# Closing a row block of a graph layer: a 32x32 turn-back on VectorE with statistics added over quadrants, in place of TensorE transposes

## The reference, cut to what matters

```python
# x: 8192 x 256, adj: 8192 x 8192, w: 256 x 256, all float32
xw  = max(sign(x), 0) @ sign(w).T
out = relu(adj @ xw)
y   = x + out
result = (y - mean(y)) / sqrt(var(y) + 1e-5)     # along the 256 columns of each row
```

## Time and profile before

| | us |
|---|---|
| three runs: median | 991.02 |
| three runs: lowest, highest | 989.96, 991.04 |
| the profiled execution | 990.72 |
| span of its instructions | 988.9 |
| TensorE busy in it | 972.6 (98%) |
| VectorE busy | 846.8 (86%) |
| GpSimd busy | 841.8 (85%) |
| ScalarE busy | 614.2 (62%) |

### The profile page before, as it was taken

The page is one execution under the profiler, slowest core; times in us unless marked ns, Lnnn a source line. Parts: engine busy times, 40 slices in busy tenths (PEclk is TensorE's granted clock), DMA queues, the critical chain, the costliest instruction groups (busy, mean ns, idle before and its releaser), DMA issues.

```text
span 988.9 us, 12529 instructions
## 1 busy us (share of the span) xinstructions
PE 972.6 (98%) x4612; PEld 810.2 (82%) x4612; DVE 846.8 (86%) x879; ACT 614.2 (62%) x657; POOL 841.8 (85%) x362
## 2 busy tenths in 40 slices
PE   5999999999999999999999999999999999999997
PEld 5978888888888888888888888888888888888886
DVE  5777988989888898988989898898988989898894
ACT  3777675665656566565665656566565656656563
POOL 3567998988889899888998889899888998889893
PEclk9999999999999999999999999999999999999999
DMA  9999999999999999999999999999999999999971
GB/s 300 348 349 326 318 314 283 323 324 285 326 287 309 283 321 312 287 316 308 287 302 298 330 287 301 310 294 317 293 316 277 310 285 322 326 287 308 320 185 43
DMA packets 296701, 294.70 MB, mean 298 GB/s; under 512 B 9664, under 2 KB 296640, under 8 KB 296640
## 3 DMA queue, kind: packets, MB, share of 16 engines
q1 hardware_dynamic: 156640, 155.21, 57.0%
q10 hardware_dynamic: 140000, 138.69, 49.8%
HBM read 285.47 MB, written 8.39 MB: 297 GB/s over the span
## 4 chain that ended last, share of the span: by engine, by line
PE 96%; DMA 1%; DVE 1%; ACT 1%; ACTq 1%; issue 0%; POOL 0%; DVEq 0%
PE ps L617 91%; PE ps L691 1%; PE ps L611 1%; DMA raw<-in_adj_dram 1%; PE ps L593 1%; PE ps L655 1%; ACTq L194 1%; ACT hi L324 0%; PE ps L583 0%; DVE turned L444 0%; POOL lo L304 0%; ACT xw L317 0%; ACTq L187 0%; PE ps L679 0%; DVE ps L444 0%
## 5 line engine op out<-in xcount | busy, mean ns | idle before, releaser
L304 POOL TENSOR_TENSOR lo<-turned,hi 128x1024 fp32r<-128x1024 f32 x351 | 838.6, 2411 | 118.3 <-ACT hi L324 114.4
L617 PE MATMUL ps<-hi,xw 128*128 128x512 f32 x1984 | 774.4, 390 | 0.5 <-ACT xw L317 0.5
L617 PE MATMUL ps<-lo,xw 128*128 128x512 f32 x1984 | 772.2, 389 | 0.0
L324 ACT ACTIVATE hi<-turned 128x1024 fp32r<-128x1024 f32 x351 | 372.6, 1062 | 254.8 <-PE ps L617 173.4
L617 PEld LDWEIGHTS ps<-hi,xw 128*128 128x128 f32 x1984 | 372.5, 188 | 77.8 <-ACT xw L317 1.1
L617 PEld LDWEIGHTS ps<-lo,xw 128*128 128x128 f32 x1984 | 372.5, 188 | 76.7
L444 DVE STREAM_TRANSPOSE turned<-raw 128x1024 f32<-128x1024 f32 x351 | 425.1, 1218 | 1.2 <-DMA raw<-in_adj_dram 1.2
L448 DVE TENSOR_TENSOR lo<-ps,hi 128x1024 fp32r<-128x1024 f32 x161 | 196.6, 1221 | 111.0 <-ACT hi L324 111.0
L324 ACT ACTIVATE hi<-ps 128x1024 fp32r<-128x1024 f32 x161 | 165.1, 1026 | 89.5 <-PE ps L617 77.2
L444 DVE STREAM_TRANSPOSE ps<-raw 128x1024 f32<-128x1024 f32 x161 | 196.4, 1220 | 3.0 <-DMA raw<-in_adj_dram 2.9
L341 ACT ACTIVATE rows<-rows,shift,rstd 128x256 f32<-128x256 f32 x62 | 36.2, 586 | 1.6 <-DVE shift L467 1.6
(11 more groups left out here) (39 smaller groups left out, 131.9 us busy)
## 6 DMA issues: line engine op xcount, KB each, us to landing
raw<-in_adj_dram SPq DMA_DIRECT2D x250, 512.0 KB, 11.0
raw<-in_adj_dram ACTq DMA_DIRECT2D x250, 512.0 KB, 12.0
rows<-in_x_dram SPq DMA_DIRECT2D x16, 512.0 KB, 10.8
out_dram<-rows SPq DMA_DIRECT2D x15, 512.0 KB, 15.9
raw<-in_adj_dram SPq DMA_DIRECT2D x12, 256.0 KB, 8.7
raw<-in_adj_dram ACTq DMA_DIRECT2D x12, 256.0 KB, 9.4
x_sb<-in_x_dram SPq DMA_DIRECT2D x10, 256.0 KB, 10.6
x_sb<-in_x_dram ACTq DMA_DIRECT2D x10, 256.0 KB, 11.1
```

Of the source, the lines that this page charges most:

```text
L304: pool.tensor_tensor(lo[:, n % RING], turned[:, ordinal(n) % TP], hi[:, n % RING].bitcast(f32), ALU.subtract).then_inc(p_los_made, 1)
L324: act.activation(hi[:, n % RING], src, ACT.Copy).then_inc(his_made, 1)
L617: return pe.matmul(acc[b % 2][a], xw[:, step, a * P:(a + 1) * P], part[:, n % RING, k * MB:(k + 1) * MB], start=(step == 0 and part is hi) ...
```

## The change

The ending of the blocks 0 to 14 is made anew; block 15 keeps its own, with its columns in another order.

- The columns of `sign_wT` are put in another order, so that half `a` of the features holds, for each quadrant q of the partitions, the columns 64q + 32a to 64q + 32a + 31. VectorE turns the sums back in 32x32 squares, in one instruction from PSUM to SBUF (u = 7). Partition (q, r) then holds a quarter (64 columns) of the rows 32t + r, for t = 0 to 15.
- At u = 8 relu and the sum with x are one instruction (128x1024, both inputs in SBUF). x is loaded by quadrants: four DMAs of 128 KB per block, two from SyncE and two from ScalarE, in runs of 256 bytes; the result is stored likewise. There are two buffers in turns: the old `rows` and a new `rows_e`.
- Statistics are first taken of 64 columns each (16 small instructions at u = 9 to 12), and then TensorE adds over the quadrants with a 128x128 matrix `quads`: means behind unit 8, variances behind unit 16, two float32 matmuls of 16 columns each. Between them VectorE has four small instructions, at u = 16, 17 and 18.
- ScalarE loses its two relus; the standard deviations come at u = 23, and 16 normalising operations of 64 columns at u = 27 to 30.
- TensorE loses the 8 transposes of each ending, and the last unit of a block runs its products in the order of the others.

The core of the diff (the tail's waits, the semaphores and the allocation of buffers are left out):

```diff
+    C4 = D // G
+    MEANS_AT, VARS_AT = 8, 16
...
+    x_quads = x.rearrange("(b t r) (q c) -> b q r t c", t=NT, r=Q, q=G)
+    out_quads = out.rearrange("(b t r) (q c) -> b q r t c", t=NT, r=Q, q=G)
...
+        def load_quads(eng, b, side):
+            if b >= 2:
+                eng.wait_ge(quads_stored[b % 2], b // 2 * G * 16)
+            elif b == 0:
+                eng.wait_ge(signs_turned, 1)
+            else:
+                eng.wait_ge(xw_made, GROUPS)
+            for q in side:
+                eng.dma_start(rows_q[b % 2][q * Q:(q + 1) * Q], x_quads[b, q]).then_inc(quads_loaded[b % 2], 16)
+
+        def store_quads(eng, b, side):
+            eng.wait_ge(blocks_done, b + 1)
+            for q in side:
+                eng.dma_start(out_quads[b, q], rows_q[b % 2][q * Q:(q + 1) * Q]).then_inc(quads_stored[b % 2], 16)
...
SyncE, for b in 1..15, for c in 0..7, behind load_chunk:
-                    if c == 2 and b >= 2:
-                        store_rows(b - 2)
-                    if c == 3:
-                        load_rows(b - 1)
+                    if c == 0:
+                        load_quads(sp, b - 1, LOWER)
+                    if c == 3 and b >= 2:
+                        store_quads(sp, b - 2, LOWER)
...
ScalarE:
             def ending(b, u):
-                if u == RING - 1:
-                    make_relu(b)
-                if u == 18:
-                    make_std(b, slice(0, MT))
-                if 22 <= u < 22 + MT:
-                    normalise(b, u - 22, u - 22 == MT - 1)
+                if u == 23:
+                    act.wait_ge(vars_summed, b + 1)
+                    act.activation(std_q[:], sum_vars, ACT.Sqrt, bias=eps[:], scale=1.0 / Q).then_inc(stds_made, 1)
+                if 27 <= u < 31:
+                    act.wait_ge(shifts_made, b + 1)
+                    for t in range((u - 27) * G, (u - 26) * G):
+                        row = rows_q[b % 2][:, t]
+                        done = act.activation(row, row, ACT.Identity, bias=shift_q[:, t:t + 1], scale=rstd_q[:, t:t + 1])
+                    if u == 30:
+                        done.then_inc(blocks_done, 1)
+                if u == 31:
+                    store_quads(act, b, UPPER)
...
+                if n % UB == 20 and n // UB < NBLK - 1:
+                    load_quads(act, n // UB, UPPER)
...
VectorE:
             def ending(b, u):
...
+                if u == 7:
+                    dve.wait_ge(units_used, (b + 1) * UB)
+                    dve.wait_ge(sums_made, b)
+                    dve.transpose(flat[0].rearrange("p (t a j) -> p a t j", t=NT, a=DH), pair[b % 2]).then_inc(sums_turned, 1)
+                if u == 8:
+                    dve.wait_ge(sums_turned, b + 1)
+                    dve.wait_ge(quads_loaded[b % 2], (b // 2 + 1) * G * 16)
+                    dve.scalar_tensor_tensor(out=rows_q[b % 2], in0=back_q, scalar=0.0, in1=rows_q[b % 2],
+                                             op0=ALU.max, op1=ALU.add).then_inc(sums_made, 1)
+                if 9 <= u < 13:
+                    dve.wait_ge(sums_made, b + 1)
+                    for t in range((u - 9) * G, (u - 8) * G):
+                        dve.bn_stats(stats_q[:, t], rows_q[b % 2][:, t]).then_inc(stats_made, 1)
+                if u == 16:
+                    dve.wait_ge(means_summed, b + 1)
+                    for e in range(2):
+                        last = dve.tensor_tensor(dev_q[:, :, e], stats_q[:, :, 1 + 3 * e], sum_means, ALU.subtract)
+                    last.then_inc(devs_made, 1)
+                if u == 17:
+                    dve.wait_ge(devs_made, b + 1)
+                    dve.tensor_tensor(sq_q[:], dev_q[:], dev_q[:], ALU.mult).then_inc(squares_made, 1)
+                if u == 18:
+                    dve.wait_ge(squares_made, b + 1)
+                    dve.scalar_tensor_tensor(out=dev_q[:], in0=sq_q[:], scalar=float(Q), in1=parts,
+                                             op0=ALU.mult, op1=ALU.add).then_inc(parts_made, 1)
...
(u == 25: reciprocal of std_q; u == 26: shift_q from sum_means and rstd_q)
...
+            def make_quads():
+                dve.wait_ge(idents_made, 2)
+                dve.tensor_reduce(quad[:], ident[:].rearrange("p (q r) -> p r q", q=G), mybir.AxisListType.X,
+                                  ALU.add).then_inc(quad_made, 1)
+                dve.wait_ge(quad_made, 1)
+                for q in range(G):
+                    last = dve.tensor_scalar(quads[:, q * Q:(q + 1) * Q], quad[:], 1.0 / (G * 2), None, ALU.mult)
+                last.then_inc(quads_made, 1)
...
+                if n == UB - 2:
+                    make_quads()
...
TensorE:
-            def turn_back(b):
...
+            def add_means(b):
+                if b == 0:
+                    pe.wait_ge(quads_made, 1)
+                pe.wait_ge(stats_made, (b + 1) * NT)
+                if b:
+                    pe.wait_ge(shifts_made, b)
+                for e in range(2):
+                    last = pe.matmul(sum_means, quads[:], stats_q[:, :, 1 + 3 * e], start=(e == 0), stop=(e == 1))
+                last.then_inc(means_summed, 1)
+
+            def add_vars(b):
+                pe.wait_ge(parts_made, b + 1)
+                if b:
+                    pe.wait_ge(stds_made, b)
+                for e in range(2):
+                    last = pe.matmul(sum_vars, quads[:], dev_q[:, :, e], start=(e == 0), stop=(e == 1))
+                last.then_inc(vars_summed, 1)
...
-                if n >= UB and n % UB == BACK_AT:
-                    turn_back(n // UB - 1)
+                if n >= UB and n % UB == MEANS_AT:
+                    add_means(n // UB - 1)
+                if n >= UB and n % UB == VARS_AT:
+                    add_vars(n // UB - 1)
```

More of the change, by code:

```diff
@@ L105, in build @@
         shift = sb("shift", [P, MT], f32)
+        quad = sb("quad", [P, Q], f32)
+        quads = sb("quads", [P, P], f32)
+        stats_q = sb("stats_q", [P, NT, 6], f32)
+        dev_q = sb("dev_q", [P, NT, 2], f32)
+        sq_q = sb("sq_q", [P, NT, 2], f32)
+        std_q = sb("std_q", [P, NT], f32)
+        rstd_q = sb("rstd_q", [P, NT], f32)
+        shift_q = sb("shift_q", [P, NT], f32)
         eps = sb("eps", [P, 1], f32)
         warm = sb("warm", [P, 1], f32)
+        rows_q = [rows_e[:], rows[:].rearrange("p m d -> p (m d)").rearrange("p (t c) -> p t c", t=NT)]
         flat = [t.rearrange("p a b -> p (a b)") for t in (relu[:], rows[:])]
@@ L117, in build @@
         acc = [[ps[:, (2 * h + a) * BANK:(2 * h + a + 1) * BANK] for a in range(DH)] for h in range(2)]
+        pair = [ps[:, 2 * h * BANK:(2 * h + 2) * BANK].rearrange("p (a t r) -> p a t r", a=DH, t=NT) for h in range(2)]
+        sum_means, sum_vars = (ps[:, b * BANK:b * BANK + NT] for b in (6, 7))
         back = ps[:, 6 * BANK:8 * BANK].rearrange("p (m d) -> p m d", m=MT)
@@ L131, in build @@
         adj_loaded = [sem(f"adj_loaded{s}") for s in range(SLOTS)]
+        quads_loaded = [sem(f"quads_loaded{i}") for i in range(2)]
+        quads_stored = [sem(f"quads_stored{i}") for i in range(2)]
         rows_loaded = sem("rows_loaded")
@@ L281, in _ @@
                              rows[:, ms[0]:ms[-1] + 1]).then_inc(rows_stored, 16)
-            sp.wait_ge(rows_stored, (NBLK + 1) * 16)
+            sp.wait_ge(rows_stored, 2 * 16)
+            for i in range(2):
+                sp.wait_ge(quads_stored[i], (NBLK - i) // 2 * G * 16)
             sp.wait_ge(tile_stored, 16)
@@ L324, in make_hi @@
                 act.activation(hi[:, n % RING], src, ACT.Copy).then_inc(his_made, 1)
[L326 to L333, removed]
             def make_std(n, ms):
-                act.wait_ge(mvs_made, n + 1)
+                act.wait_ge(mvs_made, n - NBLK + 2)
                 act.activation(std[:, ms], mv[:, ms, 1], ACT.Sqrt, bias=eps[:]).then_inc(stds_made, 1)
@@ L409, in _ @@
             dve.wait_ge(w_negs, 1)
[L410 removed]
+            dve.scalar_tensor_tensor(out=sign_w, in0=w_sb, scalar=0.0, in1=w_neg,
                                      op0=ALU.is_gt, op1=ALU.subtract).then_inc(signs_made, 1)
@@ L470, in ending @@
             def ending(b, u):
-                whole = slice(0, MT)
-                if u == 13:
-                    dve.wait_ge(relus_turned, (b + 1) * MT)
-                    dve.wait_ge(rows_loaded, (b + 1) * 16)
-                    add_rows(whole)
-                if u == 14:
-                    for m in range(MT):
-                        make_stats(b, m)
-                if u == 15:
-                    dve.wait_ge(stats_made, (b + 1) * MT)
-                if u == 16:
-                    for m in range(MT):
-                        last = make_mv(m)
-                    last.then_inc(mvs_made, 1)
@@ L485, in ending @@
-                if u == 20:
-                    make_rstd(b, whole)
-                if u == 21:
-                    make_shift(b, whole)
+                means, parts = stats_q[:, :, 1::3], stats_q[:, :, 2::3]
```

(17 more changed lines are left out.)

61 lines of the change are left out of this document (29 added, 32 removed).

## The result

| us | before | changed |
|---|---|---|
| median of the runs | 990.94 | 1042.32 |
| lowest, highest | 989.96, 991.04 | 1029.74, 1054.38 |
| profiled execution | 990.72 | 1054.38 |
| span | 988.9 | 1052.6 |
| TensorE busy | 972.6 (98%) | 998.0 (95%) |

The changed kernel is slower: ratio 1.040, 95% interval [1.0379, 1.042], some 40 us. The forecast was 988.4 (982 to 1001).

The account below looks back on a forecast made before the run. TensorE, 98% busy and 96% of the chain, was taken as the bound: 990.72 - 4.7 (transposes out, small matmuls in) + 2.1 (block 1's wait) = 988.1, plus 0.30 to the median, forecast 988.4 us, range 982 to 1001.

Parts of the forecast that it names:

- four DMA issues, behind running activations: nothing: On ScalarE: the four DMA issues it gets per block stand behind running activations and cost no time.
- DMA: On the DMA queues: 256-byte runs take 3.5 us more per block, hidden by 8.6 us that are free.
- the 9 us more of the prediction: On the DMA engines: if a 256-byte run costs 47 ns like a whole one, 12.0 us per block instead of 3.0.
- the rival built on it: DMA becomes the bound: 9 us more against about 8 free, 1 to 1.6 per block, 1003 to 1010 us; chance 0.05.
- A pair of small matmuls: On TensorE: two float32 matmuls of 16 columns cost 0.28 us with the return, two pairs 0.56 per block.
- float32 in several passes: Rival on TensorE: four passes make a pair 0.87 us, total 1006; two passes 0.95 per block, 994; chance 0.17.
- the 4.7 us to be gained: On TensorE: transposes of 0.875 us per block replaced by matmuls of 0.56, saving 4.7 us over 15 blocks.
- Block 1: VectorE comes out of block 0 late, so TensorE waits behind unit 8: 2.1 us lost, once.
- VectorE's burst: From the turn of unit 7 to the last statistic VectorE issues 13.4 us of work; no wait in steady blocks.
- 0.6 for GpSimd: In steady blocks, VectorE's relu-and-sum waits 0.6 us for a GpSimd instruction to end, leaving a margin of 0.6.
- T0: The moment at which TensorE starts a block's unit 0, from which the prediction counts a block's times.
- The sum's upper bound: Upper of the forecast sum's own bounds, 983 and 994 us, for the whole kernel.

Follow-up runs that it names:

- f3: Changed kernel with the same eight DMAs per block in runs of 4 KB instead of 256 bytes: 995.7 us, ratio 1.0043 to the kernel before.
- f2: Changed kernel with the means asked for behind unit 10 instead of 8: 1029.4 us, ratio 1.0403 to the kernel before.
- g3: Changed kernel with all loads of x in runs of 4 KB, all stores still at 256 bytes: 1009.5 us, ratio 1.0192 to the kernel before.
- f1: Changed kernel with all eight small DMAs per block issued by SyncE, none by ScalarE: 1114.5 us, from 1087 to 1134.
- h2: Changed kernel with all eight DMAs per block in runs of 512 bytes: 996.4 us, ratio 1.006 to the kernel before.
- k1: Kernel before, plus eight added DMAs of 128 KB per block in runs of 256 bytes at the change's places: 1111.4 us, from 1085 to 1123.
- j3: Changed kernel with all small DMAs on SyncE and 20 of a block's 32 adj loads on ScalarE: 1204 us, from 1152 to 1224.
- g2: Changed kernel with SyncE's small DMAs in runs of 4 KB, ScalarE's still at 256 bytes: 1096.7 us, ratio 1.1077 to the kernel before.
- h3: Changed kernel with ScalarE's four small DMAs put at units apart: 1016 us, from 1007 to 1026, ratio 1.0175 to the kernel before.
- f4: Changed kernel with the turn-back to PSUM, so relu-and-sum has one input in SBUF: 1024.5 us, ratio 1.0348 to the kernel before.

## Why the prediction was wrong

**The step that failed** is one sentence: ScalarE gets "four DMA issues, behind running activations: nothing". In the kernel before an issue took 0.32 us at the median and cost nothing. Of the four new ones the two loads took 1.7 and 2.0 at the median and up to 4.8, and the adj issues beside them up to 4.2. f3 puts 35 us on the cut of the new DMAs, and with long runs most of the stands go too: 21 issues over 1 us instead of 109. The chains of the changed kernel, f2 and g3 show the way from a stand to TensorE; what part of the 35 us takes it is not measured, since the run that freed ScalarE (f1) made adj late. The kernel before did hint at it: SyncE's issues of the same adj loads have a median of 0.93 us and reach 8.4 (shown above), so a queue can hold its issuer. I read that as harmless, since SyncE computes nothing, and did not ask what it means for the engine that does.

**DMA** was priced in the wrong currency. I took the engines' time: 3.5 us more per block, hidden by 8.6 free. About that much came. The pages of f3 and of f2 give, for the two queues (packets, MB, share of 16 engines' span):

```profile
q1 hardware_dynamic: 143680, 147.35, 53.8%
q10 hardware_dynamic: 142880, 146.56, 53.2%
```

```profile
q1 hardware_dynamic: 172480, 147.35, 54.9%
q10 hardware_dynamic: 171680, 146.56, 54.0%
```

1.070 x 994.5 = 1064 and 1.089 x 1027.5 = 1119: 55 us over 15 blocks, 3.7 per block. Some luck is in it: the middle between nothing and the 9 us more of the prediction is 4.5, not 3.5. In h2, with 512 bytes, it is 1.074 x 992.8 = 1066, as in f3. The Trainium skill, "DMA: Bandwidth & Descriptors", Specifications, puts full rate at 512 bytes and more: these three agree with it, on both sides of that length. Its rule spoke against the change, and I gave the rival built on it a chance of 0.05 and 1003 to 1010 us, since I looked only at whether the engines would be full. The time is 20 to 27 us beyond, and by another way.

**A pair of small matmuls**: 0.28 predicted, 0.47 measured, 15 x 2 x 0.19 = 5.7 us. Here the rival "float32 in several passes", in its milder form of two (0.44 decides), was right: the 4.7 us to be gained became 1.0 lost. The Trainium skill, "FP8 and Floating Point Precision", TensorE Precision Notes, has true FP32 as four passes; the profile lists two instructions per product, and what happens inside of one isn't shown.

**Block 1**: gap of 2.1 predicted, 2.2 seen once in f3, none later. The term lacked the clock behind it, 1.6.

**VectorE's burst** was about right, its start was not. With 0.6 for GpSimd the prediction has it at 14.0 us; it took 13.6 in f3 and 14.1 in the changed kernel (relu-and-sum 1.46 and 1.97 us at the median). But it was to start 1.65 us after TensorE's start of the block, as it does in f3 (1.8, the statistics at T0 + 15.4, no wait in a steady block); in the changed kernel the turn of unit 7 comes 3.3 to 7.4 us after it. So the wait behind unit 8 is lateness brought along, not a longer burst. Four normalising operations of 64 columns take 1.42 us (the changed kernel's chain, at 837.80), 0.33 from one to the next, as predicted.

**The sum's upper bound** was put too low: 990.72 + 2.9 + 2.1 + 0.3 gives 996, not 994.

With the pair at 0.47 and block 1 at 3.8 the prediction's own sum would have given 990.7 + 1.0 + 3.8 = 995.5, and f3 measured 995.7 (993.9 to 996.3). So it describes the kernel without short runs, and even that isn't faster. The time was given back in two places: small float32 matmuls cost as much as the transposes, and the short runs took the rest.

**What stays open.** What part of the 35 us goes by way of ScalarE's stands, and why a queue holds its issuer. The count of packets seems to be part of it: in f1 a held queue takes 512 in about 2.5 us, and in such units SyncE and ScalarE have 18 and 16 per block in the kernel before, 18 and 18 in h2, 20 and 20 in the changed one, 22 and 20 in k1, 24 and 16 in f1, which is nearly the order of their times. But j3 has 20 and 20 again and takes 1204, and g2, with fewer, 1097. So how the two queues act on each other isn't settled, nor the parts of length and count in the step from 512 to 256 bytes. Between h3 and the kernel before remain some 17 us; I didn't find a place for ScalarE's small DMAs that gives them back. No version tried beats the kernel before.

## What to carry to other kernels

Before an engine that computes is given a DMA, look at how long issues of the same kind take on the other queue, median and most: an issue isn't a fixed 0.3 us, and where it holds the engine, its stream stands. Keep runs at 512 bytes or more when a layout is chosen for its arithmetic; here 256 instead of 512 cost 3.4%. Price small float32 matmuls by what a pair adds to a block's period, not by the columns.

## What the runs showed that I had not expected

- An issue of adj can hold ScalarE for 4.2 us (6.9 in g2); the same instruction takes 0.318 at the median.
- Here lateness of one queue was not cured by moving its DMAs to another: with all small ones on SyncE 1114 us, with adj moved over in exchange 1204.
- A gap of 2.2 us on TensorE cost 3.8: the 64 products behind it took 16.23 us instead of 14.65.
- VectorE waits for GpSimd even for tiny instructions with both inputs in SBUF. GpSimd and VectorE in one block of f3, start, duration, what:

```profile
415.49 12.00 POOL L340 TENSOR_TENSOR lo<-turned,hi 128x1024 fp32r<-128x1024 f32 x5 [0.34 <-ACT hi L360]
```

```profile
420.14 0.19 DVE L529 TENSOR_TENSOR sq_q<-dev_q 128x32 f32<-128x32 f32 x1
...
421.42 1.33 DVE L533 SCALAR_TENSOR_TENSOR dev_q<-sq_q,stats_q 128x32 f32<-128x32 f32 x1
```

GpSimd's second and third instruction end at 415.49 + 2 x 2.40 = 420.29 and at 422.69. The squares end just behind the one, at 420.33, the parts just behind the other, at 422.75. In all 15 blocks the parts end 0.06 us behind the end of GpSimd's running instruction; they take 1.33 to 1.36 us where it has that much left, and 1.95 where it has more, in block 1. The Trainium skill, "SBUF — State Buffer", Terms, has a port pair that the two engines share and that is locked for a whole instruction; the trace agrees, as in the earlier trace rows, and so does f4, where one input is in PSUM.
